# Where the key building of the expert choice keeps its mark, and when the next similarities are computed

## The chip, the cores and the metric

The kernel runs on one core of a Trainium2 chip. Times are microseconds (us) on the device for the whole kernel, launch to end. The core has a matrix engine (PE, with its weight loads shown apart as PEld), a vector engine (DVE), an activation engine (ACT), GpSimd (POOL) and a queue engine that issues transfers (SP). SBUF is the big on-chip memory ("mem" in the profile), PSUM the accumulator memory of eight banks ("bank"). POOL instructions of this kernel work on SBUF alone.

## The reference, cut to what matters

```python
x = x + xattn(layernorm(x), ctx, ctx)        # 4 x 512 tokens, 256 wide, 16 heads
x = x + ffn(layernorm(x))
# ffn, for every token and each of 8 heads:
q   = (x_norm @ wq).reshape(B, T, 8, 2, 128)
sim = einsum('bthpd,hkpd->pbthk', q, keys)   # 2 x 64 similarities a head
s1, i1 = top_k(sim[0], 16);  s2, i2 = top_k(sim[1], 16)
all_scores = s1[..., :, None] + s2[..., None, :]
all_idx    = i1[..., :, None] * 64 + i2[..., None, :]
final_scores, pk = top_k(all_scores, 16);  final_idx = all_idx at pk
hidden = gelu(einsum('btd,bthkd->bthk', x_norm, down[final_idx])) * relu(final_scores)
out    = einsum('bthk,bthkd->btd', hidden, up[final_idx])
```

The kernel does not gather experts. It builds, for 256 tokens at a time, a dense table of coefficients over all 4096 experts by one-hot products, computes `hidden` and `out` densely, and multiplies the two with the coefficients.

## The kernel before

The 2048 tokens are 16 tiles of 128 tokens. An attention stage (to about 455 us) also chooses the experts of tiles 0 to 4 on the side (`NA = 5`). The expert stage that follows works on chunks of 256 tokens, k = 0 to 7, each in 16 slots q; k = -1 is its prologue. A slot of each engine holds, in a fixed order:

- PE: `hidden` of slot q (four fp32 products into bank 4 or 7), `coefficients` of slot q - 1 (48 small one-hot products), `output` of slot q - 2, and in some slots `turn_numbers`, `turn_output` (after chunk ends) and one half of `similarities` for a later tile (two products of 512 columns into bank 0, as much column work as `hidden`).
- DVE: `one_hots` for the coefficients (L1315 and L1318), in every second slot the product of gelu and coefficients (L1332), in slot 4 `add_residual` (L1339), and then about two tasks of the expert choice of a tile.
- POOL: `weigh` (L848, which waits for DVE's L1315), in every second slot its own product (L855), and for the choice `candidates` (L714), `expert_numbers` (L723, L727) and `weight_parts` (L735 to L745).
- ACT: gelu (L1009 and L1011), the copy of the coefficients out of PSUM (L1020), of the similarities (L996), of a chunk's output (L1025).

The choice of a tile on DVE is a list of 17 tasks: eight `search` (the two top 16 of a head), four `choose` (top 16 of the sums of two heads), one `keys`, four `extract` (the chosen in order of a key), then `decode`. `spread` lays the tasks out evenly: some 1.9 tasks a slot for tiles 9 to 15 (k = 2 to 5), about two for tiles 5 to 8 (k = 0 and 1). The table `now` in `walk` tells the engines what else hangs on a slot: "mult" lists the slots in which `similarities` and its copy `take_sim` run for the next tile, the slot of a certain task and the slot after it.

`make_keys` is four DVE instructions over 128 x 400 elements (8 heads x 50 sums): L1192 marks the chosen places (a value where `c1` is GONE, times a code of the place), L1193 puts the low bits of the sum with the expert number, L1196 builds the weight key from the high bits and the mark, L1198 adds the mark to the expert key. All their operands are in SBUF: `cand`, `c1`, `cidx`, `pcode`, `taken`, `wkey`, `ikey`. `key` is raised at L1196; POOL waits on it before it overwrites `cand` and `cidx` for the next tile. Bank 0 holds a tile's similarities until ACT's copy to SBUF; bank 5 holds the numbers 0 to 127 (128 columns) that `one_hots` compares with, copied there by DVE at L1302 before the stage.

Of the kernel before, what the change touches and what calls it, by code (L numbers as in the profile page):

```python
# [5 lines left out]
F32 = mybir.dt.float32  # L6
# [3 lines left out]
ALU = mybir.AluOpType  # L10
# [6 lines left out]
P = 128  # L17
# [11 lines left out]
FH, NK, TOPK = 8, 64, 16  # L29
# [11 lines left out]
NC = sum(ROWS)  # L41
# [7 lines left out]
GONE = float(np.float32(-3.0e38))  # L49
PBITS, LOW = 25, 7  # L50
# [16 lines left out]
def build(nc, x, ctx_in, Wq, bq, Wk, bk, Wv, bv, Wo, bo, norm_w, wq, keys, down, up, out):  # L67
    ctx = ExitStack()
    with ctx:
        def sem(name):  # L70
            return ctx.enter_context(nc.semaphore(name))
# [12 lines left out]
        psum = [ctx.enter_context(nc.psum_tensor(f"bank{i}", [P, 512], F32)) for i in range(8)]  # L84
# [15 lines left out]
        cand, c1, taken, wkey, ikey = (mem.take(FH * NC).rearrange("p (h n) -> p h n", h=FH) for _ in range(5))  # L100
        cidx = mem.take(FH * NC, I32).rearrange("p (h n) -> p h n", h=FH)
        pcode = mem.take(FH * NC, I32).rearrange("p (h n) -> p h n", h=FH)
# [9 lines left out]
        mark = mem.at  # L112
# [73 lines left out]
        NA = 5  # L186
# [4 lines left out]
        def spread(n_tiles, first, steps):  # L191

            n = n_tiles * len(TASKS)
            return [(first + t * (steps - first) // n, t // len(TASKS), *TASKS[t % len(TASKS)]) for t in range(n)]

        def choice_start(tile):
            return 2 * HG + 2 * tile
# [10 lines left out]
        for g in range(SLOTS):  # L208
# [16 lines left out]
            if g % 2 == 0 and g >= choice_start(0):  # L225
                tile = (g - choice_start(0)) // 2
# [72 lines left out]
        iconst = sem("iconst")  # L299
# [11 lines left out]
        key = sem("key")  # L311
# [72 lines left out]
        def at_least(eng, s, value):  # L384

            if isinstance(value, int) and value <= 0:
                return
            eng.wait_ge(s, value)
# [41 lines left out]
        def walk(k0, n_slots, t0, n_tiles, kk0):  # L430

            tasks = spread(n_tiles, 0, 16 * n_slots)
            if kk0 == -1:
                tasks = [(11 + 5 * n // FEW if n < FEW else 16 + 32 * (n - FEW) // (len(tasks) - FEW), *tasks[n][1:])
                         for n in range(len(tasks))]
            turned = t0 - 2 if kk0 in (2, 6) else t0 - 1
            for x in range(16 * n_slots):
                sl = x // 16  # L440
                kk = None if kk0 is None else kk0 + sl
                par = (0 if kk0 is None else kk0) + sl
                now = {"tasks": [(t0 + t, kind, i) for s, t, kind, i in tasks if s == x],
                       "fetch": [t0 + (t + 1) for s, t, kind, i in tasks if s == x and (kind, i) == ("search", 4)],
                       "mult": [(t0 + (t + 1), x - s) for s, t, kind, i in tasks
                                if x - s in (0, 1) and (kind, i) == ("choose", 3)],
                       "sums": [(t0 + t, 2 * i // FH) for s, t, kind, i in tasks if s + 1 == x and kind == "search" and
                                2 * (i + 1) % FH == 0],
                       "numbers": [t0 + t for s, t, kind, i in tasks if s + 1 == x and (kind, i) == ("choose", 0)],
                       "turn": [t0 + t for s, t, kind, i in tasks if s + 3 == x and (kind, i) == ("extract", 3)]}  # L450
                if x == 2 and kk0 in (2, 6):
                    now["turn"].insert(0, t0 - 1)
                if now["turn"]:
                    turned = now["turn"][-1]
                now["turned"] = turned
                yield x % 16, k0 + sl, par % 2, kk, now
# [423 lines left out]
        def _(act):  # L880
# [98 lines left out]
            for _, name, index in before:  # L979
                take(name, index)  # L980
# [73 lines left out]
        def _(dve):  # L1054
# [80 lines left out]
            def bits(ap):  # L1135
                return ap.bitcast(I32)

            steps = Steps(dve, dve_step)
# [46 lines left out]
            def make_keys(v):  # L1185

                c, w, ik = bits(cand), bits(wkey), bits(ikey)
                dve.wait_ge(cix, v * len(SEGS) + len(SEGS))  # L1190
                steps.all()
                steps.count(nc.vector.scalar_tensor_tensor(taken, c1, GONE, pcode.bitcast(F32), ALU.is_equal, ALU.mult))  # L1192
                low = steps.count(nc.vector.scalar_tensor_tensor(ik, c, (1 << LOW) - 1, cidx, ALU.bitwise_and,  # L1193
                                                                 ALU.bitwise_or))
                steps.after(low)
                nc.vector.scalar_tensor_tensor(w, c, LOW, bits(taken), ALU.logical_shift_right, ALU.bitwise_or).then_inc(key, 1)  # L1196
                dve.wait_ge(key, v + 1)
                steps.count(nc.vector.tensor_tensor(ik, ik, bits(taken), ALU.bitwise_or))  # L1198

            def extract(s):  # L1200

                if s == 0:
                    steps.all()
                both = [(k, o, h) for h in (2 * s, 2 * s + 1) for k, o in ((wkey, kA), (ikey, kB))]
                a = [steps.count(nc.vector.max(o[:, h, 0:8], k[:, h, :])) for k, o, h in both]  # L1205
                b = []
                for n, (k, o, h) in enumerate(both):
                    steps.after(a[n])
                    b.append(steps.count(nc.vector.match_replace(k[:, h, :], o[:, h, 0:8], k[:, h, :], 0.0)))  # L1209
                for n, (k, o, h) in enumerate(both):  # L1210
                    steps.after(b[n])
                    steps.count(nc.vector.max(o[:, h, 8:16], k[:, h, :]))  # L1212
# [19 lines left out]
            def choose_experts(tile, kind, i):  # L1232

                if kind == "search":
                    search(tile, i)
                elif kind == "candidates":
                    return
                elif kind == "choose":
                    choose(tile, i)
                elif kind == "keys":  # L1240
                    make_keys(tile)
                else:
                    extract(i)
                    if i == 3:
                        decode(tile)

# [18 lines left out]
            for g in range(SLOTS):  # L1265
                b, r = g // HG, g % HG
                for i in range(16):
                    if i == 0 and 1 <= g <= NG:
                        max_parts(g - 1)
                    if g < NG:  # L1270
                        n = 16 * g + i
# [28 lines left out]
            dve.wait_ge(iconst, 2)  # L1300
            dve.wait_ge(o_ev, NG)
            nc.vector.tensor_copy(psum[5][:, 0:P], iota.rearrange("p c t -> p (c t)").bitcast(F32)).then_inc(iconst, 1)  # L1302
            dve.wait_ge(iconst, 3)
            numbers = psum[5][:, 0:P].bitcast(BF16).rearrange("p (c t) -> p c t", c=P)

            def one_hots(k, par, kk, q):
# [54 lines left out]
        def _(pe):  # L1361
# [166 lines left out]
            def similarities(tile, n):  # L1528
                if n == 0:
                    pe.wait_ge(xs_ld, tile * 16 + 16)  # L1530
                at_least(pe, sim_ev, tile * 2 + (n - 2 * NA))
                for k in range(KD):
                    last = mm(psum[0][:, :], xs[:, k, :], wqk[:, k, n * 512:(n + 1) * 512], k == 0, k == KD - 1)
                last.then_inc(sim_mm, 1)
# [113 lines left out]
```

## Time and profile before

| | |
|---|---|
| median of 3 runs | 1187.69 us (1186.41 to 1188.65) |
| the profiled execution's own time | 1188.53 us |
| its span | 1186.7 us |
| PE busy | 1032.1 us, 87% of the span |
| DVE busy | 951.8 us, 80% |
| POOL busy | 640.9 us, 54% |
| ACT busy | 393.8 us, 33% |

The profiled execution took 0.8 us more than the median, and 1.8 us of it lie outside its span. The shares are means over two stages of different character: in the attention stage PE is busy some 70 to 80% of the time, in the expert stage nearly always. A busy engine is not one that sets the end by itself; what it waits for, and who waits for it, is in the waits.

### The profile page before, as it was taken

Reading aid. Unit: us, or ns where it says so; the run is one execution under the profiler, and the core shown is the slowest. Engines: PE = TensorE matmul, PEld = TensorE weight load, DVE = VectorE, ACT = ScalarE, POOL = GpSimd, SP = SyncE. Lnnn points to the kernel's source line nnn. Section 1 sums busy time; section 2 is a strip of 40 time slices with the busy share of each in tenths; the row PEclk is TensorE's granted clock in tenths of the full one; section 3 lists DMA queues with packets and bytes.
Section 4 is the critical chain, followed back from the end, with each engine's and each line's share of the span. In section 5 each row is a group of like instructions: output and inputs, shape, how many; then the busy total and the mean of one; then the engine's idle time right before and its main releaser. Section 6 shows DMA issues by size and latency. Waiting matters only on the chain.

```text
span 1186.7 us, 28163 instructions
## 1 busy us (share of the span) xinstructions
PE 1032.1 (87%) x10088; PEld 721.1 (61%) x10088; DVE 951.8 (80%) x4847; ACT 393.8 (33%) x725; POOL 640.9 (54%) x793
## 2 busy tenths in 40 slices
PE   4779989877878676479989989999999999999998
PEld 2434434323313223367878878888888878888887
DVE  4756566989998977999999899999989999953210
ACT  2246655443544353232222222222222222222211
POOL 6340340343021215567777877878777786787511
PEclk9789999888978888679999999999999999999999
DMA  5344324131221102610000000000010000010000
GB/s 169 118 146 124 116 81 127 56 112 47 90 75 43 49 7 105 246 32 6 22 21 21 22 11 26 27 11 27 7 34 22 21 16 16 26 34 8 2 18 10
DMA packets 60347, 63.82 MB, mean 54 GB/s; under 512 B 7184, under 2 KB 56592, under 8 KB 59696
## 3 DMA queue, kind: packets, MB, share of 16 engines
q1 hardware_dynamic: 60208, 62.03, 16.6%
q8 instruction: 80, 1.31, 0.5%
q14 instruction: 59, 0.48, 0.1%
HBM read 42.34 MB, written 19.66 MB: 52 GB/s over the span
## 4 chain that ended last, share of the span: by engine, by line
DVE 38%; PE 36%; POOL 12%; issue 7%; DMA 2%; ACT 2%; SPq 2%; DVEq 0%; POOLq 0%; ACTq 0%
PE bank L1363 33%; POOL mem L848 5%; DVE mem L1318 5%; DVE mem L1273 4%; DVE mem L1209 3%; PE bank L1366 3%; DVE mem L1156 2%; DVE mem L1155 2%; DVE mem L1205 2%; DVE mem L1212 2%; DVE mem L1192 2%; SPq L501 2%; DVE mem L1315 2%; POOL mem L714 1%; DVE mem L1160 1%
## 5 line engine op out<-in xcount | busy, mean ns | idle before, releaser
L1363 PE MATMUL bank<-mem 128*128 128x32 bf16 (+6 forms) x9608 | 983.7, 275 | 107.0 <-DVE mem L1273 34.1
L1363 PEld LDWEIGHTS bank<-mem 128*128 128x128 bf16 (+4 forms) x9608 | 668.8, 122 | 377.0 <-issue 172.4
L848 POOL TENSOR_TENSOR mem<-mem 128x1536 bf16<-128x1536 bf16 x123 | 339.8, 2763 | 137.6 <-DVE mem L1315 137.5
L1273 DVE TENSOR_REDUCE mem<-bank 128x1 f32<-128x512 f32 x256 | 167.8, 683 | 65.7 <-PE bank L1363 64.8
L969 ACT ACTIVATE mem<-bank 128x512 f32<-128x512 f32 x256 | 148.0, 603 | 189.7 <-PE bank L1363 188.9
L1318 DVE TENSOR_TENSOR mem<-mem,bank 128x2048 bf16<-128x2048 bf16 x128 | 155.5, 1215 | 0.0
L1020 ACT COPY mem<-bank 128x512 f32<-128x512 f32 x128 | 74.9, 585 | 120.9 <-PE bank L1363 120.8
L1366 PE MATMUL bank<-mem 128*128 128x128 f32 (+3 forms) x480 | 74.6, 287 | 44.3 <-DVE mem L1073 17.6
L855 POOL TENSOR_TENSOR mem<-mem 128x512 f32<-128x512 f32 x64 | 83.2, 1299 | 50.5 <-ACT mem L1009 50.5
L1366 PEld LDWEIGHTS bank<-mem 128*128 128x128 f32 (+3 forms) x480 | 55.1, 141 | 85.0 <-issue 37.2
L714 POOL TENSOR_TENSOR mem<-mem 128x32 f32<-128x32 f32 (+5 forms) x224 | 45.6, 241 | 105.2 <-DVE mem L1164 105.2
L1011 ACT ACTIVATE bank<-bank 128x512 f32<-128x512 f32 x64 | 37.2, 582 | 171.0 <-PE bank L1363 171.0
L1009 ACT ACTIVATE mem<-bank 128x512 f32<-128x512 f32 x64 | 38.3, 598 | 161.5 <-PE bank L1363 161.5
L1315 DVE TENSOR_TENSOR mem<-mem,bank 128x512 bf16<-128x512 bf16 x128 | 52.4, 409 | 43.0 <-PE bank L1363 39.8
L1332 DVE TENSOR_TENSOR mem<-bank,mem 128x512 f32<-128x512 f32 x64 | 43.9, 686 | 47.0 <-ACT bank L1011 39.0
L1155 DVE FIND_INDEX8 mem<-mem 128x8 uint32<-128x64 f32 x256 | 52.9, 219 | 0.0
L1156 DVE MATCH_REPLACE8 mem<-mem 128x64 f32<-128x64 f32 x256 | 51.6, 209 | 0.0
L1209 DVE MATCH_REPLACE8 mem<-mem 128x50 f32<-128x50 f32 x256 | 47.0, 196 | 0.0
L735 POOL TENSOR_TENSOR mem<-mem 128x128 f32<-128x128 f32 x16 | 7.2, 450 | 73.7 <-DVE mem L1226 73.7
L1160 DVE MAX8 mem<-mem 128x8 f32<-128x64 f32 x256 | 44.3, 215 | 0.0
L1152 DVE MAX8 mem<-mem 128x8 f32<-128x64 f32 x256 | 43.6, 212 | 0.0
L749 POOL TENSOR_SCALAR mem<-mem 128x4 f32<-128x4 f32 x4 | 0.9, 234 | 76.8 <-DVE mem L1065 76.8
(105 smaller groups left out, 785.3 us busy)
## 6 DMA issues: line engine op xcount, KB each, us to landing
mem<-parts_d SPq DMA_DIRECT2D x192, 64.0 KB, 2.2
parts_d<-mem SPq DMA_DIRECT2D x16, 384.0 KB, 2.7
mem<-in_L_ffn_expert_down SPq DMA_DIRECT2D x16, 256.0 KB, 2.9
downT_d<-mem SPq DMA_DIRECT2D x16, 256.0 KB, 3.1
mem<-downT_d SPq DMA_DIRECT2D x4, 1024.0 KB, 8.0
mem<-in_L_ffn_expert_up SPq DMA_DIRECT2D x4, 1024.0 KB, 12.2
tok_d<-mem SPq DMA_DIRECT2D x16, 160.0 KB, 1.8
mem<-tok_d SPq DMA_DIRECT2D x16, 160.0 KB, 2.4
```

Source lines behind the costliest of these rows:

```text
L848: nc.gpsimd.tensor_tensor(ow[q % 2], i0, i1, ALU.mult).then_inc(ow_rdy, 1)
L855: nc.gpsimd.tensor_tensor(gm[q % 4], gm[q % 4], coef[par][:, 2 * q:2 * q + 2, :], ALU.mult)\
L969: nc.scalar.activation(p_sb[quad % 3][:, hh, :], psum[3 + n % 2][:, :], ACT.Exp, scale=DK ** -0.5)\
L1020: nc.scalar.copy(coef[1 - par][:, :, q * TK:(q + 1) * TK], src).then_inc(c_ev, 1)
L1155: steps.count(nc.vector.max_index(i[:, h, c, 0:8], s[:, h, c, 0:8], src[c]))
L1156: cut = [steps.count(nc.vector.match_replace(left[c], s[:, h, c, 0:8], src[c], GONE)) for c in range(2)]
L1209: b.append(steps.count(nc.vector.match_replace(k[:, h, :], o[:, h, 0:8], k[:, h, :], 0.0)))
L1273: nc.vector.tensor_reduce(nmx[g % 2][:, i % TB, i // TB:i // TB + 1], psum[n % 3][:, :], AX.X, ALU.max, negate=True).then_inc(s_max, 1)
L1315: nc.vector.tensor_tensor(oj[q % 2], low.to_broadcast([P, TP, JL, PAIR]), numbers[:, 0:JL, :].unsqueeze(1).to_broadcast([P, TP, JL, PAIR]) ...
L1318: nc.vector.tensor_tensor(oh[q % 2], high.to_broadcast([P, TP, P, PAIR]), numbers.unsqueeze(1).to_broadcast([P, TP, P, PAIR]), ALU.is_equa ...
L1363: return nc.tensor.matmul(o, l, r, start=first, stop=last)
L1366: return nc.tensor.transpose(o, i, ident)
```

## The change

There are three edits.

1. In `make_keys`, for tiles 5 to 15 the mark goes to bank 0 (its first 400 columns) in place of `taken`, and the place code is read from bank 5 (50 columns beside the numbers, repeated over the heads) in place of the full `pcode` in SBUF. For tiles 0 to 4 both stay in SBUF.
2. For all tiles the four instructions stand in another order: mark; weight key from `cand` and mark; low bits of `cand` put into the mark in place; expert key from mark and `cidx`. `key` is raised at the last one, and DVE waits for it at the start of `extract`. With edit 1, each of the four then has one input in SBUF and one in PSUM, and the first and third write to PSUM. DVE copies the 50 codes to bank 5 once, beside L1302.
3. The slots of "mult" follow `extract` 0 in place of `choose` 3: the next tile's similarities are computed later, in most tiles by one slot. From tile 6 on PE waits for `key` of the tile before, since both use bank 0.

```diff
@@ walk
                         "mult": [(t0 + (t + 1), x - s) for s, t, kind, i in tasks
-                                if x - s in (0, 1) and (kind, i) == ("choose", 3)],
+                                if x - s in (0, 1) and (kind, i) == ("extract", 0)],
@@ make_keys
-                steps.count(nc.vector.scalar_tensor_tensor(taken, c1, GONE, pcode.bitcast(F32), ALU.is_equal, ALU.mult))
-                low = steps.count(nc.vector.scalar_tensor_tensor(ik, c, (1 << LOW) - 1, cidx, ALU.bitwise_and,
+                if isinstance(v, int) and v < NA:
+                    mark, code = taken, pcode.bitcast(F32)
+                else:
+                    mark = psum[0][:, 0:FH * NC].rearrange("p (h n) -> p h n", h=FH)
+                    code = place_code.unsqueeze(1).to_broadcast([P, FH, NC])
+                at = steps.count(nc.vector.scalar_tensor_tensor(mark, c1, GONE, code, ALU.is_equal, ALU.mult))
+                steps.after(at)
+                steps.count(nc.vector.scalar_tensor_tensor(w, c, LOW, bits(mark), ALU.logical_shift_right, ALU.bitwise_or))
+                low = steps.count(nc.vector.scalar_tensor_tensor(bits(mark), c, (1 << LOW) - 1, bits(mark), ALU.bitwise_and,
                                                                  ALU.bitwise_or))
                 steps.after(low)
-                nc.vector.scalar_tensor_tensor(w, c, LOW, bits(taken), ALU.logical_shift_right, ALU.bitwise_or).then_inc(key, 1)
-                dve.wait_ge(key, v + 1)
-                steps.count(nc.vector.tensor_tensor(ik, ik, bits(taken), ALU.bitwise_or))
-
-            def extract(s):
+                nc.vector.tensor_tensor(ik, bits(mark), cidx, ALU.bitwise_or).then_inc(key, 1)
+
+            def extract(v, s):
 
                 if s == 0:
+                    dve.wait_ge(key, v + 1)
                     steps.all()
@@ before the expert stage, on DVE
-            dve.wait_ge(iconst, 3)
+            nc.vector.tensor_copy(psum[5][:, 256:256 + NC], pcode[:, 0, :].bitcast(F32)).then_inc(iconst, 1)
+            dve.wait_ge(iconst, 4)
+            place_code = psum[5][:, 256:256 + NC]
@@ similarities, on PE
                 if n == 0:
                     pe.wait_ge(xs_ld, tile * 16 + 16)
+                    if tile > NA:
+                        pe.wait_ge(key, tile)
```

## Rows read from the trace of the kernel before

**Rows 1.** The page: busy time of each engine in the whole span.
```profile
PE 1032.1 (87%) x10088; PEld 721.1 (61%) x10088; DVE 951.8 (80%) x4847; ACT 393.8 (33%) x725; POOL 640.9 (54%) x793
```
**Rows 2.** Windows: stretch, length, busy time by engine, PE clock, DMA.
```profile
516.00:1040.00 524.00, 501.40 (x6284) 424.92 (x6283) 505.66 (x2969) 136.54 (x231) 405.05 (x446) 0.99 0.07 20
1040.00:1187.00 147.00, 139.08 (x1365) 122.13 (x1363) 40.12 (x74) 31.10 (x53) 69.18 (x40) 0.99 0.04 13
```
**Rows 3.** Waits of PE in 516 to 1040: total us, times, longest.
```profile
PE bank L1363 <- DVE mem L1332: 9.9, 11, 2.6
PE bank L1363 <- ACT mem L1025: 5.8, 5, 1.2
PE bank L1363 <- DVE mem L1315: 2.3, 1, 2.3
PE bank L1366 <- DVE mem L1339: 2.1, 1, 2.1
```
**Rows 4.** Waits of DVE, and of POOL, in 516 to 1040.
```profile
DVE mem L1171 <- POOL mem L714: 10.2, 5, 3.1
DVE mem L1192 <- POOL mem L727: 4.5, 6, 1.0
DVE mem L1315 <- PE bank L1363: 0.7, 2, 0.6
...
POOL mem L848 <- DVE mem L1315: 102.6, 63, 4.4
```
**Rows 5.** Groups of DVE in 516 to 1040: busy us, mean ns.
```profile
L1332 DVE TENSOR_TENSOR mem<-bank,mem 128x512 f32<-128x512 f32 x48 | 32.9, 685 | 0.0
L1192 DVE SCALAR_TENSOR_TENSOR mem<-mem 128x400 f32<-128x400 f32 x11 | 23.9, 2176 | 4.9 <-POOL mem L727 4.5
L1193 DVE SCALAR_TENSOR_TENSOR mem<-mem 128x400 int32<-128x400 int32 x11 | 14.1, 1286 | 0.0
L1196 DVE SCALAR_TENSOR_TENSOR mem<-mem 128x400 int32<-128x400 int32 x11 | 6.3, 575 | 0.4
```
**Rows 6.** Groups of DVE: L1192 of tiles 1 to 4; two more forms with a bank.
```profile
L1192 DVE SCALAR_TENSOR_TENSOR mem<-mem 128x400 f32<-128x400 f32 x4 | 2.3, 568 | 0.0
...
L1100 DVE TENSOR_TENSOR mem<-bank,mem 128x256 f32<-128x256 f32 x16 | 6.8, 424 | 0.5
...
L1302 DVE COPY bank<-mem 128x128 f32<-128x128 f32 x1 | 0.3, 282 | 0.0
```
**Rows 7.** Timeline around the keys of tile 15: start, length, what.
```profile
1024.75 0.58 ACT L996 COPY mem<-bank 128x512 f32<-128x512 f32 x1 [2.95 <-PE bank L1363]
...
1026.47 0.60 ACT L1009 ACTIVATE mem<-bank 128x512 f32<-128x512 f32 x1 [1.14 <-PE bank L1363]
1026.99 2.76 POOL L848 TENSOR_TENSOR mem<-mem 128x1536 bf16<-128x1536 bf16 x1
1027.06 3.12 DVE L1192 SCALAR_TENSOR_TENSOR mem<-mem 128x400 f32<-128x400 f32 x1 [0.87 <-POOL mem L727]
...
1031.20 0.58 ACT L996 COPY mem<-bank 128x512 f32<-128x512 f32 x1 [2.95 <-PE bank L1363]
```
**Rows 8.** Timeline of PE: its long waits after the keys of tile 5.
```profile
561.84 9.72 PE L1363 MATMUL bank<-mem 128*128 128x256 f32 x128 [2.61 <-DVE mem L1332]
...
606.09 1.97 PE L1363 MATMUL bank<-mem 128*128 128x256 f32 x8 [1.41 <-DVE mem L1332]
609.30 7.91 PE L1363 MATMUL bank<-mem 128*128 128x32 bf16 x120 [1.24 <-issue]
...
703.57 7.38 PE L1363 MATMUL bank<-mem 128*128 128x32 bf16 x112 [2.35 <-DVE mem L1315]
...
811.29 0.44 PE L1366 MATMUL bank<-mem 128*128 128x128 bf16 x5 [2.11 <-DVE mem L1339]
...
998.65 1.56 PE L1363 MATMUL bank<-mem 128*128 128x256 f32 x6 [1.29 <-DVE mem L1332]
...
1048.51 6.11 PE L1363 MATMUL bank<-mem 128*128 128x32 bf16 x112 [1.29 <-issue]
```

More of the change, by code:

```diff
@@ L1242, in choose_experts @@
                 else:
-                    extract(i)
+                    extract(tile, i)
                     if i == 3:
```

## The prediction

> **What bounds the kernel now.** The page comes first [rows 1]: PE has the largest share, DVE is next. Such a share says little about a kernel of two stages, so the next view is the busy time by stretch [rows 2]. From 516 to 1040 us, where tiles 5 to 15 are chosen, PE is busy 501 of 524 us and DVE 506 of 524; POOL has room (405). From 1040 on the choice is over, DVE is busy 40 of 147 us, and PE 139 of 147. So the tail is PE's alone, and in the middle two engines run side by side, each almost full. Whatever PE waits there is lost for good: the tail can't give it back, and it can't swallow it either.
>
> The third view is who waits for whom in that middle stretch. PE waits for DVE 9.9 + 2.3 + 2.1 = 14.3 us in these groups [rows 3]; another 5.8 us it waits for ACT's copy of a chunk's output, which the change doesn't touch. DVE waits for PE 0.7 us in all, and for POOL 10.2 + 4.5 us [rows 4]. POOL's waits at L848 are all for DVE's own one-hots [rows 4]; POOL has no row there that waits for PE. So DVE is a chain that nearly never stops, with POOL hanging on it, and PE runs at its own pace except where it catches up with that chain. Time taken from DVE becomes time of the kernel, up to what PE waits for it. That is the reading on which all of the rest stands.
>
> **What the key instructions cost.** L1192 takes 568 ns in tiles 1 to 4 [rows 6], but 2176 ns in the mean of the 11 tiles of the expert stage; L1193 takes 1286 there, L1196, of the same shape, 575 [rows 5]. The timeline shows why. At tile 15, POOL's L848 starts at 1026.99 and takes 2.76 us, to 1029.75; L1192 starts at 1027.06 and takes 3.12 us, to 1030.18 [rows 7]. The DVE instruction does not run slower, it stands until POOL's is done and then needs its usual time less what overlaps. Its two inputs are both in SBUF. L1332, which also has two inputs but one in a bank, ran 48 times in the same stretch, with the same POOL instructions about, at 685 ns in the mean [rows 5]. The same form at half the length, L1100, takes 424 [rows 6]: 261 ns for 256 elements, 1.02 ns each, and a fixed part of 163. At 400 elements this line gives 571 ns, where L1192 undisturbed has 568. So the bank form runs as if POOL were not there, and costs no more than the SBUF form when that one is left alone.
>
> The Trainium skill says the same of the cause: "SBUF — State Buffer", section on the two separate sides, has GpSimd and a DVE instruction with two SBUF inputs share one pair of ports under an exclusive lock held for the whole instruction. Rows 5 and 7 agree with it.
>
> **Edit 1 and 2, on DVE.** The excess is 23.9 - 11 x 0.57 = 17.6 us at L1192 and 14.1 - 11 x 0.57 = 7.8 at L1193, 25.4 in all, 2.3 us a tile. After the change no key instruction has two SBUF inputs, so I take all of it away. The new forms themselves are not in the trace. Lower bound: the 568 ns of today. Nearest rows: a bank as input adds 3 ns (571 against 568, above), a bank as output adds nothing (L1302, 282 ns for 128 elements, where the line gives 294). The combination, and codes that are read again for every head, has no row; if each of the four instructions took the 685 ns of the 512-element form, the nearest row above, it would be 0.11 x 4 x 11 = 5 us more in all. I take 0.57 us each, and keep 20 to 25 us as the range of what DVE saves. The reordering has as many waits between instructions as before (two), so it costs nothing on DVE. `key` comes one instruction later (0.57 us); behind it stand only POOL's sums for the next tile, which come after a good part of the next searches, so nothing waits. In the attention stage (tiles 0 to 4) the four instructions keep two SBUF inputs and their count: nothing. The copy of the codes is at most L1302's 0.28 us once, at the start of the stage, where DVE is about to make the first one-hots: I book 0.2 us lost.
>
> A rule that speaks against the change: the Trainium skill, "VectorE: DVE Perf Modes", section on the TRN2 errata, gives a fixed part of 58 cycles for SBUF sources and 120 for PSUM. By it each of 44 instructions would be 65 ns dearer, an estimate of 2.8 us in all, and the DVE saving 22.6 us. The 571 and 568 ns above do not bear it out.
>
> **From DVE to the end.** DVE's saving S grows by 2.3 us a tile, PE can only gain where it waited. So I run along PE's waits and cap them by S. After tiles 5 and 6, S is 4.6; PE waited 2.61, 1.41 and 1.24 us [rows 8] and some 0.7 in shorter pieces of the 9.9 us in rows 3, about 5.9: it gains 4.6. After tiles 7 and 8, S is 9.2; PE's 2.35 at 703 [rows 8] and 1.0 in short pieces are freed: 8.0. After 9 and 10, S is 13.8, the 2.11 at 811 goes: 10.1. Tiles 11 to 13 free some 0.7 of short pieces: 10.8. Tiles 14 and 15 free 1.29 and 1.29 (the last lies just past 1040; its L848 comes late after the decoding of tile 15): 13.4. Less the 0.2 at the start, 13.2 us. S ends at 25 us, so from tile 9 on the saving is larger than what PE can use, and the rest turns into DVE waiting for PE. That is also why a dearer PSUM form, even 5 us in all, takes only about 2 off the sum (it bites in tiles 5 to 8).
>
> **Edit 3, on PE.** The similarities are the same work later, so their own length stays. The copy L996 begins as they end and the next gelu begins as `hidden` ends: 1026.47 - 1024.75 = 1.72 us for `hidden` [rows 7], and a half of the similarities has as many columns, so 1.72 as well. New is PE's wait for `key`. At tile 15 PE would come to the first half at 1031.20 - 1.72 (its own length) - 1.72 (the half that stood a slot earlier and has moved) = 1027.8 us; the keys, begun at 1027.06, would be done at 1027.06 + 4 x 0.57 = 1029.3: a wait of 1.5 us, if DVE is no earlier than today against PE. Keys and `extract` 0 stand in the same slot for six of the 11 tiles, in the others the keys are a slot ahead and there is room of a slot. By tile 15 DVE has a lead that it lacks today, and the wait vanishes; at tile 5 there is no lead yet, and something like 1 us may be waited, but PE waits 2.6 us for DVE two slots on anyway, so it takes at most a few tenths. I book 0. The next tile's first search comes two slots or more after `extract` 0, after the copy of the similarities in every tile, so DVE has no new wait. SP's load of `xs` hangs on the fourth search and on similarities long done; nothing moves in its queue.
>
> The sum: 13.2 us off the profiled execution of 1188.5 gives 1175.3; it lay 0.8 above the median, so about 1174.5 for the median. The bookings at 0 all err to one side; I say 1175.
>
> **Rivals.**
>
> *The forecast (0.58):* DVE's saving carries on from tile to tile, PE loses nearly all its waits for DVE, 1171 to 1178.
>
> *POOL ties DVE down (0.22).* DVE waits 11 times for POOL [rows 4]. If these waits grow by as much as DVE is early, each tile's saving reaches only the PE waits before the next such place. For it: six of these waits stand right at the keys. Against: POOL itself waits for DVE's one-hots, so it comes forward with DVE. It would free the 3.3 us after tile 5, 2 after tile 6, 0.5 after tiles 7 and 8, 2.1, 0.7 and 2.6 later, 11 us, less key waits of 1 to 1.5 us in the six tiles of one slot in so far as they come to light, say 4: 7 us, so 1181.
>
> *More than the waits (0.08).* PE's waits as inferred are the least of it; a slot stretched by a late semaphore is not counted. If 17 us go, 1171 or below.
>
> *The hold stays (0.07).* If a bank output or one SBUF input were held by POOL as well, DVE keeps its 2176 ns, and the time stays: 1187 to 1188. L1332's mean speaks against it for a bank as input; that 48 of them ran free is much. But L1302 is the only row that writes a bank, and it ran once.
>
> *PE waits for the keys (0.05), the other side.* The wait of 1.5 us worked out at tile 15 would have to be there in every tile and not be taken from PE's other waits: 11 x 1.5 = 16.5 us against 13.2 gained gives 1191. It decides from 1.2 us a tile on. For it: PE is in order, and behind the similarities stand the next `hidden` and with it gelu. Against: five tiles have a slot of room, and a DVE that leads by 2 us or more has the keys done.
>
> **Range and chances.** What a measurement can tell from no change is about 0.2%, 2.4 us. The first three cases are faster: 0.58 + 0.22 + 0.08 = 0.88; the hold gives the same; the last is slower. The range goes from 1170 to 1182, which holds the forecast, the POOL case with its key waits, and most of the larger gain; the forecast's own is 1171 to 1178.
>
> **What the profile after would show.** The four key instructions in the expert stage at about 570 ns each in every tile, none near 3 us. PE's waits for L1332, L1315 and L1339 in the middle stretch down from 14 us to 2 or less. DVE's wait for PE up from 0.7 us to 5 to 10, its waits for POOL no smaller. PE's wait for the key instruction near 1 us at tile 5 and nothing later. The steps between gelus in the tail as before. Wrong would be: key instructions over 650 ns, or new waits of PE at bank 0 in many tiles, or DVE's waits for POOL grown by more than PE's waits shrank.

## The result and the profile after

| | before | after |
|---|---|---|
| median | 1187.28 us (1186.41 to 1188.65, 4 runs) | 1171.34 us (1170.15 to 1171.8, 4 runs) |
| ratio | | 0.9863, 95% interval 0.9847 to 0.9878 |
| the profiled execution's time and span | 1188.53, 1186.7 us | 1170.15, 1168.1 us |

The kernel is 15.9 us faster. The point forecast was 1175; the measured time lies in the range, and inside the likeliest case's own 1171 to 1178 at its lower edge.

First the page of the kernel after: the span, and busy time by engine.

```profile
span 1168.1 us, 28180 instructions
PE 1027.3 (88%) x10088; PEld 720.7 (62%) x10088; DVE 925.9 (79%) x4848; ACT 393.9 (34%) x725; POOL 639.1 (55%) x793
```

DVE lost 951.8 - 925.9 = 25.9 us of busy time, against 25.4 expected; PE and POOL kept theirs to within 5 us [rows 1].

The groups of DVE in the stretch 514 to 1022 us, which holds the choice of tiles 5 to 15, show all four key instructions (busy us, mean ns). They answer to [rows 5].

```profile
L1197 DVE SCALAR_TENSOR_TENSOR bank<-mem,bank 128x400 f32<-128x400 f32 x11 | 6.4, 577 | 2.7 <-POOL mem L727 2.1
L1203 DVE TENSOR_TENSOR mem<-bank,mem 128x400 int32<-128x400 int32 x11 | 6.3, 574 | 0.4
L1200 DVE SCALAR_TENSOR_TENSOR bank<-mem,bank 128x400 int32<-128x400 int32 x11 | 6.3, 572 | 0.0
L1199 DVE SCALAR_TENSOR_TENSOR mem<-mem,bank 128x400 int32<-128x400 int32 x11 | 6.3, 570 | 0.4
```

The timeline around the keys of tile 5 shows them run beside POOL's L848, where before the first one stood.

```profile
537.50 2.75 POOL L848 TENSOR_TENSOR mem<-mem 128x1536 bf16<-128x1536 bf16 x1
537.56 0.58 DVE L1197 SCALAR_TENSOR_TENSOR bank<-mem,bank 128x400 f32<-128x400 f32 x1 [1.03 <-POOL mem L727]
538.18 0.57 DVE L1199 SCALAR_TENSOR_TENSOR mem<-mem,bank 128x400 int32<-128x400 int32 x1
538.66 0.57 DVE L1200 SCALAR_TENSOR_TENSOR bank<-mem,bank 128x400 int32<-128x400 int32 x1
539.27 0.57 DVE L1203 TENSOR_TENSOR mem<-bank,mem 128x400 int32<-128x400 int32 x1
...
539.95 0.67 PE L1371 MATMUL bank<-mem 128*128 128x512 f32 x1 [1.05 <-issue]
```

L1197 begins 0.06 us after POOL's instruction and is through 2 us before it. The last row is the price of the third edit: a matmul of 512 fp32 columns is a similarity, and PE waited 1.05 us at bank 0 until the last key instruction was done at 539.84. The profile writes "issue" for it, since it finds no other releaser.

Who waits for whom, PE first, in the same stretch. It answers to [rows 3].

```profile
PE bank L1371 <- ACT mem L1025: 5.8, 5, 1.2
PE bank L1371 <- DVE mem L1340: 3.0, 2, 2.5
PE bank L1371 <- issue: 1.3, 2, 1.1
PE bank L1371 <- DVE mem L1326: 0.6, 1, 0.6
PE bank L1371 <- DVE mem L1323: 0.4, 1, 0.4
```

And DVE, which answers to [rows 4].

```profile
DVE mem L1171 <- POOL mem L714: 10.2, 5, 3.1
DVE mem L1323 <- PE bank L1371: 9.0, 13, 1.6
DVE bank L1197 <- POOL mem L727: 2.1, 4, 1.0
```

The list of before (516 to 1040 us) ends in two more groups, which the 14.3 us of the prediction leave out:

```profile
PE bank L1363 <- issue: 1.5, 2, 1.2
PE bank L1363 <- DVE mem L1318: 0.8, 1, 0.8
```

With L1318, PE's waits for DVE went from 15.1 to 4.0 us. Of the 4.0, 3.1 (2.5 at L1340, 0.6 at L1326) come before tile 5's keys, where nothing has changed yet; before, 3.3 of the 15.1 did. DVE's wait for PE went from 0.7 to 9.0 us. The roles have changed: from 733 us on, in chunk 2, DVE waits for PE again and again, and PE sets the pace. The chain that ended last says the same; before, PE had 36% and DVE 38% of it.

```profile
PE 67%; DVE 18%; POOL 4%; issue 4%; ACT 2%; DMA 2%; SPq 1%; DVEq 0%; ACTq 0%; POOLq 0%
```

**Where the 18.6 us of span came from.** DVE's copy of the numbers to bank 5 marks the start of the expert stage. It began at 455.49 us before and at 453.33 after, though the attention stage holds the same work.

```profile
453.33 0.28 DVE L1308 COPY bank<-mem 128x128 f32<-128x128 f32 x1
453.53 0.20 DVE L1309 COPY bank<-mem 128x50 f32<-128x50 f32 x1
```

In the fourteen profiles of this study that start lies anywhere from 451.8 to 458.7 us, so 2.2 us of the difference are the attention stage's own scatter. From that copy to the end of the span it is 731.2 us before, 714.8 after, and 714.7 when the changed kernel was profiled again. I call that length the expert stage below and read the experiments by it, beside the timed ratio. The change takes 16.4 us off it.

The length has a scatter of its own, which has to be taken out first. PE's first 64 matmuls of the stage, in the profile after and in that of the run with the similarities after extract 1:

```profile
455.21 4.88 PE L1371 MATMUL bank<-mem 128*128 128x256 f32 x64 [0.58 <-ACT mem L922]
456.70 6.45 PE L1371 MATMUL bank<-mem 128*128 128x256 f32 x64 [0.17 <-ACT mem L922]
```

In five of the fourteen profiles (marked * in the table below) the granted clock of PE was 0.65 or 0.66 in the first 8 us after the copy, in the other nine 1.00. In the five these matmuls took 6.43 to 6.49 us instead of 4.88 or 4.89, and DVE begins the keys of tile 5 86.2 to 86.3 us after the copy instead of 84.2 to 84.3. Variants of both kernels are among the five, and none of the edits changes the work there, so these 2.0 us belong to the execution and not to an edit. The last column of the table leaves them out: it counts from the start of tile 5's first key instruction to the end of the span. The change takes 16.5 us off that length (647.0 to 630.5).

### The profile page after: what moved, and what is told of

Read it like the earlier page. It is cut to its first block, busy times and chain, and to the rows that moved or that the text cites. A ratio compares the mean times of both kernels' runs of the same rounds, so it can differ in the third digit from the quotient of the medians.

```text
span 1168.1 us, 28180 instructions
## 1 busy us (share of the span) xinstructions
PE 1027.3 (88%) x10088; PEld 720.7 (62%) x10088; DVE 925.9 (79%) x4848; ACT 393.9 (34%) x725; POOL 639.1 (55%) x793
## 3 DMA queue, kind: packets, MB, share of 16 engines
q1 hardware_dynamic: 60208, 62.03, 16.5%
## 4 chain that ended last, share of the span: by engine, by line
PE 67%; DVE 18%; POOL 4%; issue 4%; ACT 2%; DMA 2%; SPq 1%; DVEq 0%; ACTq 0%; POOLq 0%
PE bank L1371 64%; DVE mem L1279 4%; PE bank L1374 3%; DVE mem L1326 1%; SPq L501 1%; DVE mem L1215 1%; DVE mem L1073 1%; DMA parts_d<-mem 1%; DVE mem L1155 1%; DVE mem L1156 1%; ACT mem L969 1%; POOL mem L766 1%; POOL mem L762 1%; DVE mem L1218 1%; DVE mem L1211 1%
## 5 line engine op out<-in xcount | busy, mean ns | idle before, releaser
L848 POOL TENSOR_TENSOR mem<-mem 128x1536 bf16<-128x1536 bf16 x123 | 339.5, 2761 | 122.9 <-DVE mem L1323 122.7
L1326 DVE TENSOR_TENSOR mem<-mem,bank 128x2048 bf16<-128x2048 bf16 x128 | 155.2, 1213 | 0.0
L714 POOL TENSOR_TENSOR mem<-mem 128x32 f32<-128x32 f32 (+5 forms) x224 | 45.6, 241 | 104.6 <-DVE mem L1164 104.6
L1340 DVE TENSOR_TENSOR mem<-bank,mem 128x512 f32<-128x512 f32 x64 | 43.7, 683 | 47.0 <-ACT bank L1011 39.0
```

What stands on the lines that cost most here:

```text
L848: nc.gpsimd.tensor_tensor(ow[q % 2], i0, i1, ALU.mult).then_inc(ow_rdy, 1)
L1326: nc.vector.tensor_tensor(oh[q % 2], high.to_broadcast([P, TP, P, PAIR]), numbers.unsqueeze(1).to_broadcast([P, TP, P, PAIR]), ALU.is_equa ...
```

## The experiments

Ratios are to the kernel before, on the same chip, with the 95% interval. "Stage" is the expert stage as just defined, "from keys 5" the length from tile 5's first key instruction to the end, from one profile each. Lengths are compared by the last column.

| run | median us | ratio (interval) | stage us | from keys 5, us |
|---|---|---|---|---|
| before | | 1 | 731.2 | 647.0 |
| changed, again | 1170.83 | 0.9860 (0.9836 to 0.9884) | 714.7 | 630.5 |
| mark and codes in SBUF | 1196.62 | 1.0056 (1.0030 to 1.0081) | 741.0 * | 654.8 |
| codes in SBUF | 1184.34 | 0.9967 (0.9951 to 0.9983) | 728.5 | 644.2 |
| before, codes in a bank | 1182.99 | 0.9949 (0.9932 to 0.9967) | 728.7 * | 642.4 |
| changed, four more on DVE | 1188.07 | 1.0002 (0.9986 to 1.0018) | 731.5 | 647.3 |
| changed, two more on DVE | 1179.24 | 0.9928 (0.9902 to 0.9954) | 721.4 | 637.1 |
| changed, similarities after choose 3 | 1218.41 | 1.0251 (1.0221 to 1.0281) | 762.1 * | 675.9 |
| changed, similarities after extract 1 | 1171.99 | 0.9871 (0.9848 to 0.9894) | 716.6 * | 630.4 |
| changed, output copy first | 1166.80 | 0.9814 (0.9786 to 0.9841) | 708.1 | 623.9 |
| before, output copy first | 1185.23 | 0.9974 (0.9961 to 0.9988) | 729.7 * | 643.4 |
| output copy first, decode in a bank | 1165.11 | 0.9817 (0.9799 to 0.9835) | 708.1 | 623.9 |
| output copy first, similarities after extract 1 | 1163.96 | 0.9802 (0.9783 to 0.9821) | 706.7 | 622.5 |

The theory on trial: a DVE instruction with two SBUF inputs is held while a POOL instruction runs; the bank operands end that, and the saved DVE time reaches the end as far as PE waited for DVE. Its rivals: the later place of the similarities brings the gain; the hold has another cause; DVE time doesn't count.

### The changed kernel again

> The changed kernel once more, beside the next three on the same chip. Every theory: 1170 to 1173, ratio to the kernel before 0.984 to 0.988.

It came out as expected.

### Edits 2 and 3 alone

```diff
-                if isinstance(v, int) and v < NA:
+                if True:
                     mark, code = taken, pcode.bitcast(F32)
```

> The changed kernel with the mark and the codes in SBUF for all tiles (edits 2 and 3 alone). Theory (the gain is the hold that key instructions with two SBUF inputs suffer from POOL): the hold is back, 20 to 28 us over the 11 tiles on the four key instructions, PE waits for DVE about 14 us again, and the time is that of the kernel before or up to 3 us above it for PE's new waits for the keys: 1186 to 1190. Rival (the later place of the similarities brings the gain, since PE's 3.4 us of similarities now cover the extraction): the hold is back in the rows but the time stays at 1172 to 1177.

The hold is back: L1197 and L1199 have 23.0 and 13.5 us in the stretch 514 to 1050, 23.9 more than undisturbed.

```profile
L1197 DVE SCALAR_TENSOR_TENSOR mem<-mem 128x400 f32<-128x400 f32 x11 | 23.0, 2094 | 3.1 <-POOL mem L727 2.6
L1199 DVE SCALAR_TENSOR_TENSOR mem<-mem 128x400 int32<-128x400 int32 x11 | 13.5, 1228 | 0.4
```

But the kernel is slower than before by 3.6 to 9.6 us, and from tile 5's keys on by 7.8 us, more than the 3 us at most that I had allowed. I had also expected PE to wait for DVE's one-hots and products again; it waits at bank 0 instead. The timeline of PE, its longest waits:

```profile
547.09 3.75 PE L1371 MATMUL bank<-mem 128*128 128x512 f32 x4 [5.07 <-issue]
...
642.93 7.55 PE L1371 MATMUL bank<-mem 128*128 128x512 f32 x70 [2.62 <-issue]
...
737.86 12.43 PE L1371 MATMUL bank<-mem 128*128 128x512 f32 x77 [3.30 <-issue]
...
1036.68 13.55 PE L1371 MATMUL bank<-mem 128*128 128x512 f32 x130 [2.83 <-issue]
```

These are similarities (512 columns), in tiles 5, 7, 9 and 15, which have the keys and extract 0 in one slot; tile 13 adds 2.18 us. A part of the loss is PE's clock: the granted clock fell to 0.50, the lower of its two levels (1.2 GHz), in stretches of 3 to 7 us about the waits of 5.07, 3.30, 2.18 and 2.83 us, and stood at 1.00 after that of 2.62. So the wait of PE for the keys, the rival with the other sign, is real as soon as the keys are held. The later place gives nothing by itself; that rival is refuted.

### Codes in SBUF, mark in bank 0

```diff
-                    code = place_code.unsqueeze(1).to_broadcast([P, FH, NC])
+                    code = pcode.bitcast(F32)
```

> The changed kernel with the mark in bank 0 but the place codes read from SBUF, so that of the four key instructions the first alone has two SBUF inputs (output in a bank). Theory (each instruction is held by its own two SBUF inputs, whatever its output): the first is held as before, 15 to 18 us over 11 tiles, the other three run at 0.57 us; DVE saves 7 to 9 of the 25 us and PE gains most of that, so 1178 to 1182. Rival (a bank output frees an instruction): the first runs at 0.58 us too and the time is 1171 to 1173.

```profile
L1197 DVE SCALAR_TENSOR_TENSOR bank<-mem 128x400 f32<-128x400 f32 x11 | 23.2, 2109 | 3.2 <-POOL mem L727 2.7
...
L1199 DVE SCALAR_TENSOR_TENSOR mem<-mem,bank 128x400 int32<-128x400 int32 x11 | 6.3, 571 | 0.4
```

Two SBUF inputs and a bank output: held as before, 2109 ns. One SBUF input and a bank output (L1200 after): free. So it is the inputs, as theory has it. The time is 2 us above the expected 1178 to 1182: the hold now stands ahead of PE's wait for the keys, and PE waited 3.62, 2.03, 2.37 and 1.99 us at the similarities of tiles 5, 7, 9 and 15. After the first and the third of these its granted clock stood at 0.50 for a while.

### The kernel before, with the codes in a bank

```diff
-                steps.count(nc.vector.scalar_tensor_tensor(taken, c1, GONE, pcode.bitcast(F32), ALU.is_equal, ALU.mult))
+                if isinstance(v, int) and v < NA:
+                    code = pcode.bitcast(F32)
+                else:
+                    code = place_code.unsqueeze(1).to_broadcast([P, FH, NC])
+                steps.count(nc.vector.scalar_tensor_tensor(taken, c1, GONE, code, ALU.is_equal, ALU.mult))
```

> The kernel before, with the codes of L1192 read from bank 5 and nothing else changed (old order, mark in SBUF, similarities where they were). Theory (POOL's instruction holds whichever DVE instruction with two SBUF inputs comes while it runs): L1192 is free at 0.57 us, but L1193 right behind it meets the same POOL instruction and is held for what is left, 2.0 to 2.6 us where L1192 stood 3.1; over the tiles at most 0.5 to 1 us a tile is saved, 1181 to 1186. Rival (the hold belongs to the first instruction alone): the whole 17.6 us excess of L1192 goes, and the time falls to 1174 to 1178.

The groups of DVE, then its timeline at tile 5:

```profile
L1197 DVE SCALAR_TENSOR_TENSOR mem<-mem 128x400 int32<-128x400 int32 x11 | 21.8, 1983 | 0.0
L1200 DVE SCALAR_TENSOR_TENSOR mem<-mem 128x400 int32<-128x400 int32 x11 | 11.1, 1007 | 0.4
...
L1196 DVE SCALAR_TENSOR_TENSOR mem<-mem,bank 128x400 f32<-128x400 f32 x11 | 6.3, 570 | 5.0 <-POOL mem L727 4.6
```

```profile
539.66 0.57 DVE L1196 SCALAR_TENSOR_TENSOR mem<-mem,bank 128x400 f32<-128x400 f32 x1 [1.05 <-POOL mem L727]
540.14 2.62 DVE L1197 SCALAR_TENSOR_TENSOR mem<-mem 128x400 int32<-128x400 int32 x1
```

The first instruction is free, at 570 ns where it had 2176 [rows 5]. The second inherits the hold: 1983 ns where it had 1286; and L1200, the third, has 1007 where it had 575. DVE saves 17.6 at the first and loses 7.7 and 4.8 at the next two: 5 us net of the 25. From tile 5's keys on the kernel is 4.6 us shorter. The theory's expectation held (1181 to 1186, measured 1182.99). It follows that freeing the first alone is not enough. The order in edit 2 gives each of the four a bank input; the fourth was at 574 or 575 ns in every run, so none shows that it needed one.

### More load on DVE

```diff
                 if s == 0:
                     dve.wait_ge(key, v + 1)
                     steps.all()
+                    if v >= NA:
+                        for _ in range(4):                      # 2 in the other run
+                            at = steps.count(nc.vector.scalar_tensor_tensor(taken, c1, GONE,
+                                             place_code.unsqueeze(1).to_broadcast([P, FH, NC]), ALU.is_equal, ALU.mult))
+                            steps.after(at)
```

> The changed kernel with four more DVE instructions of the new kind (one SBUF and one bank input, output to the unused mark in SBUF) a tile, behind the keys: 11 x 4 x 0.6 = 26 us of plain DVE time, as much as the hold cost, and nothing that touches POOL. Theory (only DVE's time counts, PE gains or loses by the capped sum): PE waits for DVE 12 to 16 us again and the time is 1184 to 1189. Rival (the gain is from POOL or PE being freed, and DVE has room to spare): 1171 to 1176.

> The changed kernel with two more DVE instructions of the new kind a tile (half of the load of the run with four): 11 x 2 x 0.57 = 12.5 us of DVE time. Theory (capped running sum: DVE saves 1.2 us a tile against the kernel before, PE gains it until its own waits are used up): the capped sum gives 10 to 11 of 13.4 us, so only 3 to 5 us are lost of 12.5: 1174 to 1177. Rival (DVE time goes to the end one for one): half of what four more cost, 8 us, 1179.

Four more cost 44 x 0.569 = 25.0 us of DVE time and bring back the length of before (647.3 against 647.0 us from tile 5's keys), without any hold. So DVE time by itself is enough to account for the whole gain; the load stood behind the keys, near the place of the saving, and no run put it elsewhere. The waits of PE for DVE in the four-more kernel, 500 to 1060 us:

```profile
PE bank L1377 <- DVE mem L1346: 7.0, 8, 2.5
...
PE bank L1377 <- DVE mem L1329: 2.2, 2, 1.2
PE bank L1380 <- DVE mem L1353: 1.6, 1, 1.6
PE bank L1377 <- DVE mem L1332: 1.2, 1, 1.2
```

They add up to 12.0 us, the lower edge of the 12 to 16 expected.

Two more, 12.5 us, cost 6.6 us of stage. The median time, 1179.24, is at the rival's figure and above my 1174 to 1177. But against the kernel before it reads otherwise: a DVE saving of 25.4 - 12.5 = 12.9 us gains 9.8 us, and the capped sum, run with 1.2 us a tile, gives about 10 for it. The curve bends (12.9 saved: 9.8; 25.4 saved: 16.4), which one for one does not. What I had wrong was the upper end, from which I counted down.

### The place of the similarities

```diff
-                                if x - s in (0, 1) and (kind, i) == ("extract", 0)],
+                                if x - s in (0, 1) and (kind, i) == ("choose", 3)],    # or ("extract", 1)
```

> The changed kernel with the similarities where they were in the kernel before (after choose 3), but still behind the keys of the tile before, as bank 0 demands. PE then stands at bank 0 until the keys, a slot ahead of its present place. Theory (the later place is needed by the wait on the keys, not for a gain of its own): PE waits 2 to 4 us at the keys of most tiles, 1180 to 1195. Rival (the place matters little, as DVE leads): 1171 to 1175.

> The changed kernel with the similarities one task later still (after extract 1). PE waits 1.05 us for the keys at tile 5 and about 0.7 us in all at tiles 6, 7 and 9 in the changed kernel. Theory (these waits are all that the new wait costs, and it is small): they vanish, 1 to 1.7 us are gained, 1169 to 1171. Rival (the wait at tile 5 was taken from a later wait of PE for DVE, and the searches now wait for their similarities): no gain or a loss, 1171 to 1174.

At the old place the kernel is 45 us longer than the changed one from tile 5's keys on, and the time well past the 1180 to 1195 expected. From 500 to 1060 us PE waits 44.8 us under "issue". Three of the 13 waits, 11.2 us, lie in the prologue, as in every profile; the ten others, 33.6 us, are at the similarities, up to 6.9 at once (tile 5). About these PE's granted clock fell to 0.50 in six stretches of 3 to 10 us, which costs on top of the waits. DVE waits 41.5 us for PE. The place is the condition for edit 1: whoever takes bank 0 for the mark must move the similarities.

```profile
PE bank L1371 <- issue: 44.8, 13, 6.9
```

After extract 1 the stage reads 1.9 us longer than after extract 0, but all of that is the slower start of this profile: from tile 5's keys on the two are equal (630.4 and 630.5 us), and by time they can't be told apart. The 1.05 us at tile 5 did go, but no gain followed; PE waits more elsewhere, for instance 0.90 us before a block of coefficients at 586.87, where the changed kernel has 0.26. (That 0.26, which the expectation counts as a wait for keys, is none: the row begins with 32-column matmuls, not with 512. It and the 0.90 both end 0.10 us behind the end of a `weigh` of POOL, L848, to which POOL comes straight from the choice's L714 to L727.) So the rival's "no gain" came out, and its first reason fits the rows: what PE no longer waits at tile 5 it waits later, for POOL (0.6 us more at 586.87) and for DVE (0.73 us at 675.98, where the changed kernel has 0.41). The loss of 1.9 us that a later expectation counts with is not there.

### ACT's output copy first

```diff
@@ run of ACT
+                    if q == 2 and on(kk, 1, 8):
+                        take_out(k)
                     if on(kk, 0, 7):
                         gelu(k * 16 + q, q)
...
-                    if q == 2 and on(kk, 1, 8):
-                        take_out(k)
```

PE's largest remaining wait in the expert stage is the one for L1025, 1.16 us a chunk, the copy that frees bank 6. PE begins `hidden` of slot 2 meanwhile, and ACT waits for that with its gelu before it copies.

> The changed kernel with ACT's copy of a chunk's output (L1025) ahead of the gelu of slot 2 instead of behind it and behind the copy of the coefficients. PE waits 1.16 us for that copy in each of the chunks 1 to 7. Theory (after the change PE alone sets the expert stage, so a PE wait outside the choice counts in full): 7 x 1.16 = 8 us gained, 1162 to 1165. Rival (DVE is just behind PE and takes its place as the bound, as in the first chunks): 1166 to 1170, with PE waits for DVE grown.

> The kernel before with ACT's output copy first, as control. The same edit shortened the changed kernel's expert stage by 6.7 us. Theory (in the kernel before DVE sets the pace of the first chunks, so there PE's saved 1.16 us turn into waits for DVE): 3 to 5 us gained, 1182 to 1184. Rival (PE's waits add up whatever DVE does): 6.7 to 8 us, 1179 to 1180.

In the changed kernel the stage falls by 6.7 us to 708.1 (6.6 from tile 5's keys). That is less than the 8 expected: PE is ahead again, and at the keys of tiles 5, 7 and 9 it waits:

```profile
545.32 14.88 PE L1371 MATMUL bank<-mem 128*128 128x512 f32 x144 [1.06 <-issue]
...
636.00 4.17 PE L1371 MATMUL bank<-mem 128*128 128x512 f32 x32 [1.42 <-issue]
...
727.18 13.15 PE L1371 MATMUL bank<-mem 128*128 128x512 f32 x136 [1.14 <-issue]
```

The time (1166.8) misses the expected 1162 to 1165 and lies in the rival's range, with an attention stage that took until 458.7 in the profile; but PE's waits for DVE have not grown as the rival has it, those for the keys have. In the kernel before, the same edit gains 3.6 us from tile 5's keys on, within the 3 to 5 expected, and 2.5 us of median time, a little less (0.9974, an interval of 0.9961 to 0.9988). The rest of PE's saving is swallowed. PE's waits in the stretch 500 to 1060 show it: the one for L1025 is gone, and those for DVE have grown, at L1332 from 9.9 and at L1315 from 2.3 [rows 3] to

```profile
PE bank L1363 <- DVE mem L1332: 11.2, 9, 2.6
PE bank L1363 <- DVE mem L1315: 3.8, 2, 2.3
```

The same PE saving is worth 3.6 us in the kernel where DVE sets the pace of the first chunks and 6.6 us in the changed one. This control shows the change of roles better than any share of busy time.

### Two additions to it

```diff
+                wA_of = wA if v < NA else psum[5][:, 320:320 + P].bitcast(I32)
-                wa = steps.count(nc.vector.tensor_scalar(wA, a, (1 << PBITS) - 1, LOW, ...
+                wa = steps.count(nc.vector.tensor_scalar(wA_of, a, (1 << PBITS) - 1, LOW, ...
```

> The changed kernel with the output copy first, and the first instruction of decode (L1227, one SBUF input, SBUF output, 227 ns at its median, 1271 at its longest while POOL ran) writing to free columns of bank 5. Theory (that instruction is held by POOL too, and a bank operand frees it): it takes 0.2 to 0.3 us in every tile of the expert stage; 2 to 3 us of DVE time, of which PE gets at most 1: 1163 to 1168. Rival (its long ones have another cause): the 1.27 us stay.

> The changed kernel with ACT's output copy first and the similarities after extract 1. With the output copy first PE is ahead and waits 1.06, 1.42 and 1.14 us for the keys of tiles 5, 7 and 9. Theory: these three go, but the searches of tile 6, two tasks behind, wait for the similarities, as in the run with extract 1 alone (1.9 us longer expert stage): 0 to 2 us either way of the run with the output copy first, 1163 to 1169. Rival: 3 us gained, 1161 to 1163.

The decode instruction is no longer held (295 ns in the mean of 11, 510 in the changed kernel), but the next one, L1230, which had 219, now inherits:

```profile
L1230 DVE TENSOR_SCALAR mem<-mem 128x128 int32<-128x128 int32 x11 | 4.9, 448 | 0.0
L1228 DVE TENSOR_SCALAR bank<-mem 128x128 int32<-128x128 int32 x11 | 3.2, 295 | 1.5
```

5.6 + 2.4 = 8.0 us became 8.1, and the stage stayed at 708.1. It is the second case of a hold that passes to the next instruction; here nothing at all was gained.

The output copy first with the similarities after extract 1 has the shortest stage, 706.7 us (1.4 less than with the output copy alone), and a median of 1163.96 us, in the expected 1163 to 1169. Its interval (0.9783 to 0.9821) lies below that of the changed kernel (0.9847 to 0.9878), so it beats both kernels; from the run with the output copy alone it can't be told apart.

## Why the prediction was right, point by point

**What bounds the kernel.** Confirmed. Four more instructions bring the old length back, half of them part of it, and the control with ACT's copy shows that a part of PE's own savings is swallowed where DVE lags. Of the signs named for the profile after, three did not come as written: PE's waits for the three groups are 3.4 us and not 2 or less, since the text overlooked that 2.5 of them lie before tile 5's keys; DVE's waits for POOL shrank; and tile 7 has a small wait of PE for the keys. The steps between gelus in the tail are as before (4.74 and 3.45 us).

**The hold.** Confirmed with its cause. L1197 with two SBUF inputs stands 2109 ns even with a bank output, 577 with one. The section on the two sides of SBUF in the Trainium skill's page "SBUF — State Buffer" describes just this, two SBUF inputs against a POOL instruction. The Trainium skill's 58 and 120 cycles ("VectorE: DVE Perf Modes", section on the TRN2 errata), by which each new form would be 65 ns dearer, is not borne out: 570 to 577 ns against 568 to 575. The excess taken away was 25.4 us expected, 25.9 measured as DVE busy time of the whole span.

**The capped sum** is the step that was mis-sized: 13.2 us against 16.4 of stage. The starts of ACT's gelus say where. In slot 1 of chunk 0 they come 2.2 us earlier than before, the attention stage's difference, and from slot 2 of chunk 6 on 18.6 us, so the steps between hold all of the 16.4. Through tiles 5 and 6 they gain 5.6 us where the sum had 4.6; then 4.1 where it had 3.4, 2.2 where it had 2.1 (tiles 9 and 10), 1.4 where it had 0.7, and 3.2 where it had 2.6.

A first part of the miss is the cap. The sum let S grow by the mean of 2.3 us a tile, but L1192 and L1193 took 3.12 and 1.63 us at tile 5 and 1.42 and 1.65 at tile 6. Less 0.57 for each, that is 3.6 and 1.9, together 5.5 us and not 4.6, just where the cap counted; 5.6 were gained.

The second part is that PE's idle rows are not all that a wait costs. From tile 5's keys on they add up to 14.7 us before and 2.1 after, 12.6 less, without those for L1025. The largest piece beyond them is at chunk 2, slot 2, around the wait of 2.35 us [rows 8]. Two gelus, before:

```profile
701.26 0.60 ACT L1009 ACTIVATE mem<-bank 128x512 f32<-128x512 f32 x1 [2.96 <-PE bank L1363]
...
709.79 0.58 ACT L1011 ACTIVATE bank<-bank 128x512 f32<-128x512 f32 x1 [4.18 <-PE bank L1363]
```

A slot without extra work takes 4.74 us from gelu to gelu, this one 8.53: 3.8 more. The same slot after has

```profile
692.63 0.60 ACT L1009 ACTIVATE mem<-bank 128x512 f32<-128x512 f32 x1 [2.96 <-PE bank L1371]
...
697.94 0.58 ACT L1011 ACTIVATE bank<-bank 128x512 f32<-128x512 f32 x1 [2.98 <-PE bank L1371]
```

5.31, so 3.2 us were gained, where the rows of PE's wait show 2.35 before and 0.39 after, 2.0 less. The other 1.3 us are PE's clock. The view of windows of the kernel before (stretch, length, busy time by engine, PE clock, DMA), and PE's row after:

```profile
703.90:707.30 3.40, 3.40 (x47) 2.95 (x44) 3.40 (x22) 0.58 (x1) 3.40 (x2) 0.50 0.00 0
```

```profile
692.99 6.11 PE L1371 MATMUL bank<-mem 128*128 128x32 bf16 x112 [0.39 <-DVE mem L1323]
```

Before, PE stood for 2.35 us, and then its granted clock was 0.50, the lower of its two levels (1.2 GHz), for 3.4 us. The row that begins there holds the same 112 matmuls, but took 7.38 us [rows 8] against 6.11. After the change the clock stays at 1.00 there, and everywhere from 530 to 1110 us. A wait before it was as long (2.61 us at 561.84), and the clock stood at 1.00 behind it, so the length of a wait alone does not tell. About the six other long waits of rows 8 the step from gelu to gelu gave back 0.1 to 0.3 us more than the row shows. The profile models the ends of matmuls, which may be why; no run tests it.

The third rival, "more than the waits", named the kind of the error and put 17 us to it; it had 0.08 of the chances, and the truth lies between it and the forecast. The prediction had rounded its time up, to 1175, for the terms that it booked at 0; what was measured lay the other way.

**PE's wait for the keys.** 1.05 us at tile 5, as said ("near 1 us at tile 5"), and 0.3 at tile 7 in its step from gelu to gelu, which has no row of its own. Right in the changed kernel, but by a thinner margin than the text gave: with held keys the kernel with edits 2 and 3 is 7.8 us longer than the one before, and with the similarities a slot earlier the changed kernel loses 45 us, a part of both by the lower clock that followed PE's waits. The rival had its place and its tiles right; it was held off by edit 1 alone.

**POOL as an anchor.** DVE's waits for the candidates (L714) stayed at 10.2 us to the digit, so they come forward with DVE, as argued. Those at L727 fell from 4.5 to 2.1 us, where I said they would be no smaller: where PE holds DVE back at the one-hots, POOL has probably caught up by the keys. The run with four more instructions fits that: DVE waits for PE 0.2 us there, and the waits at L727 are 4.5 us again.

**DVE's wait for PE** of 5 to 10 us: 9.0.

## What to carry to other kernels

A DVE instruction far above its usual time beside a busy POOL is standing, not working; read its minimum against its mean, and give it a bank operand in place of one SBUF input. Free the whole row of such instructions, since the next one of its kind takes over the hold. When PE's waits go, look at its granted clock beside its idle rows. And before you value a saving on one of two nearly full engines, add a known load to it and see whether the time comes back: it prices the saving without any theory of its cause.

## What the runs showed of the hardware that was not expected

The place where a hold is charged moves: freed at L1192, it went to the next two instructions (1286 to 1983 ns and 575 to 1007 ns); freed at decode's first (510 to 295 ns), it went to the one behind it (219 to 448 ns). A `tensor_scalar` with a single SBUF input and SBUF output is held too (up to 1271 ns, 227 at its median). With its output in a bank it was not (294 to 295 ns in all of 11, for 128 elements), at a price of 68 ns.

The clock of PE that was granted differed between executions of the same work: 0.66 in the first 8 us of the expert stage in five profiles, 1.00 in nine, and everything behind came 2.0 us later. From 530 to 1110 us it fell to 0.50 once in the kernel before (704 to 707 us, behind a wait of 2.35 us) and not at all in the changed one.

The attention stage, the same work in all fourteen profiles, ended between 451.8 and 458.7 us. Differences under 3 us are read better from a stage of one profile than from whole times, but only from a point behind which both profiles had the same start, and with the clock of both beside it.
